# Selective scan: spreads of delta*x for four steps as four row-tiled matmuls, product with B in SBUF, decays in place in delta's ring

## What is computed

```python
deltaBC = einsum('bld,od->blo', x, W_bc)          # 64 ranks, 32 B, 32 C
dt = einsum('blr,dr->bld', deltaBC[..., :64], W_dt)
delta = softplus(dt + b_dt)
def step(h, inp):                                 # h: [b, 512, 32]
    delta_t, B_t, C_t, u_t = inp
    dA = exp(delta_t[:, :, None] * A[None])
    dBu = (delta_t * u_t)[:, :, None] * B_t[:, None, :]
    h = dA * h + dBu
    y_t = einsum('bdn,bn->bd', h, C_t)
    return h, y_t
y = scan(step) + x * D_param
```

## Time and profile before

| | |
|---|---|
| median of 3 runs | 1846.84 us (1846.28 to 1851.75) |
| the profiled execution | 1851.74 us, of it 1850.0 from the first to the last instruction |
| TensorE (PE) busy | 1758.8 us, 95% |
| VectorE (DVE) busy | 1252.1 us, 68% |
| ScalarE (ACT) busy | 1190.2 us, 64% |
| GpSimd (POOL) busy | 1194.2 us, 65% |
| mean granted TensorE clock | 0.987 of full speed |
| the scan's stage | from about 560 to 1665 us |

### The profile page before, as it was taken

The page is one execution under the profiler, slowest core; times in us unless marked ns, Lnnn a source line. Parts: engine busy times, 40 slices in busy tenths (PEclk is TensorE's granted clock), DMA queues, the critical chain, the costliest instruction groups (busy, mean ns, idle before and its releaser), DMA issues. The chain is left out here.

```text
span 1850.0 us, 26792 instructions
## 1 busy us (share of the span) xinstructions
PE 1758.8 (95%) x9472; PEld 1134.4 (61%) x9472; DVE 1252.1 (68%) x1336; ACT 1190.2 (64%) x1775; POOL 1194.2 (65%) x932
## 2 busy tenths in 40 slices
PE   7898989889989999999999999998999999999998
PEld 5666666566756556555555656554656566667886
DVE  2524252433119999789888999887999999993212
ACT  5453443498857777787767777676776767656443
POOL 4634345255617887789976997789987888772111
PEclk9999999999999999999999999999999999999999
DMA  7443323487938988789776997777878777865652
GB/s 250 133 127 96 125 76 131 134 284 249 324 121 288 314 306 274 232 287 325 242 243 214 329 318 255 243 246 263 279 262 296 249 263 273 290 237 166 210 193 91
DMA packets 159222, 427.29 MB, mean 231 GB/s; under 512 B 30992, under 2 KB 54096, under 8 KB 158704
## 3 DMA queue, kind: packets, MB, share of 16 engines
q1 hardware_dynamic: 159088, 425.57, 68.3%
HBM read 356.30 MB, written 69.21 MB: 230 GB/s over the span
## 5 line engine op out<-in xcount | busy, mean ns | idle before, releaser
L1837 POOL TENSOR_TENSOR q_or_raw_or_h_times_c<-h_states,c_rep 128x512 f32<-128x512 f32 x293 | 376.5, 1297 | 82.1 <-DVE h_states L1730 53.0
L1609 ACT ACTIVATE decay<-delta_on_states,a_neg 128x512 f32<-128x512 f32 x512 | 350.9, 716 | 23.9 <-DMA delta_on_states<-delta 22.3
L1715 DVE TENSOR_TENSOR du_spread_in_d_b<-du_spread_in_d_b,b_rep 128x1024 f32<-128x1024 f32 x256 | 310.9, 1215 | 56.1 <-PE du_spread_in_d_b L1434 55.6
L1730 DVE TENSOR_TENSOR_SCAN h_states<-decay,h_last,du_spread_in_d_b 128x512 f32<-128x512 f32 x256 | 318.4, 1270 | 7.1
L1837 POOL TENSOR_TENSOR h_times_c_rest<-h_states,c_rep 128x512 f32<-128x512 f32 x219 | 281.2, 1295 | 63.3 <-DVE h_states L1730 40.4
L1730 DVE TENSOR_TENSOR_SCAN h_states<-decay,du_spread_in_d_b 128x512 f32<-128x512 f32 x256 | 302.7, 1209 | 13.9 <-ACT h_last L1614 6.9
L1789 POOL TENSOR_TENSOR h_lo<-v_or_silu_in_h_lo,h_hi 128x512 fp32r<-128x512 f32 x128 | 166.1, 1298 | 177.0 <-ACT h_hi L1515 176.8
L111 PE MATMUL y_or_aux<-h_hi,w 128*128 128x512 f32 x468 | 223.0, 476 | 11.8 <-POOL h_lo L1789 10.5
L1434 PE MATMUL du_spread_in_d_b<-stack,selectors 96*128 96x512 bf16 x512 | 201.1, 393 | 0.3 <-DVE h_states L1730 0.3
L1680 DVE TENSOR_TENSOR v_or_silu_in_h_lo<-v_or_silu_in_h_lo,up_or_scores 128x512 f32<-128x512 f32 x128 | 86.6, 677 | 145.3 <-PE up_or_scores L113 126.6
L1515 ACT CAST h_hi<-v_or_silu_in_h_lo 128x512 fp32r<-128x512 f32 x128 | 78.9, 616 | 164.6 <-DVE v_or_silu_in_h_lo L1680 164.5
(11 more groups left out here) (235 smaller groups left out, 3862.0 us busy)
## 6 DMA issues: line engine op xcount, KB each, us to landing
delta_on_states<-delta SPq DMA_DIRECT2D x256, 512.0 KB, 5.6
w<-w_split SPq DMA_DIRECT2D x112, 512.0 KB, 5.6
attn_w_hi_or_x_hi_w<-w_split SPq DMA_DIRECT2D x112, 512.0 KB, 5.3
attn_w_lo_or_x_lo_w<-w_split SPq DMA_DIRECT2D x112, 512.0 KB, 5.2
w_split<-w_presplit_hi_lo SPq DMA_DIRECT2D x32, 512.0 KB, 3.5
w_presplit_hi_lo<-in_w13b SPq DMA_DIRECT2D x32, 256.0 KB, 3.6
w_split<-attn_w_hi_or_x_hi_w SPq DMA_DIRECT2D x8, 1024.0 KB, 6.9
w_split<-attn_w_lo_or_x_lo_w SPq DMA_DIRECT2D x8, 1024.0 KB, 6.8
```

The costliest lines, as they stand in the source:

```text
L1609: act.activation(da[:, s % ND], dring[:, s % NR], ACT.Exp, scale=a[:, column(s):column(s) + 1]).then_inc(s_da, 1)
L1715: dve.tensor_tensor(both, both, brep[:, tile_of(s // SPO) % 2].unsqueeze(1).to_broadcast([P, 2, TT]), ALU.mult).then_inc(s_db, 1)
L1730: dve.tensor_tensor_scan(hs[:, s % NH], da[:, s % ND], uu[:, s % NU], initial, ALU.mult, ALU.add).then_inc(s_hs, 1)
L1837: pool.tensor_tensor(hc[s % NC_], hs[:, s % NH], crep[:, tile_of(s // SPO) % 2], ALU.mult).then_inc(s_hc, 1)
```

## The change

- The spreads of four steps become four matmuls of 24 rows (three parts of 8), each at a row tile of its own (`tile_position=(j * 32, 0)`), into the four banks, issued together one tick ahead of the first of the four steps. They wait for the products of the four steps before, no longer for scans. `stack` is laid out anew: 12 loads per 32 steps instead of 3.
- The product with B goes from PSUM to a new ring `db` of four in SBUF; the scan reads both of its inputs from SBUF. The second product of a quad is made one step later.
- The decay is made in place in delta's ring, which grows from 6 to 10; the ring `da` goes. Loads of delta wait for scans instead of decays.
- The sum over states is issued ahead of the tick's FFN matmuls instead of ahead of their second half, right behind the spreads.
- The selectors are smaller, and the split of W2 uses two slots instead of three, with two stores instead of one and other ticks.

```diff
-PRE_TICK = (34, 58, 66, 74, 82) + tuple(126 + 22 * i for i in range(NC - 5))
+PRE_TICK = (34, 58, 70, 82) + tuple(126 + 20 * i for i in range(NC - 4))
...
-    ND, NU, NH, NC_, NR, LAG = 6, 4, 6, 7, 6, 4
-    W13, RH = 2, 6
+    NU, NH, NC_, NR, LAG = 4, 6, 7, 10, 4
+    W13, RH, LOAD_AHEAD = 2, 6, 8
...
-        da = p.sb("decay", [P, ND, TT])
+        db = p.sb("d_b", [P, NU, TT])
...
                 def pre_load(c):
                     if c:
-                        sp.wait_ge(s_bo, c)
+                        sp.wait_ge(s_bs, 32 * c)
                     sp.dma_start(pre[:, 0], w2b[:, c]).then_inc(s_bl, 16)
 
                 def pre_store(c):
                     sp.wait_ge(s_bo, c + 1)
-                    sp.dma_start(w2x[1, c // HC, :, :, c % HC].rearrange("m p s t -> p m (s t)"),
-                                 pre_hl.rearrange("p m s t -> p m (s t)")).then_inc(s_bs, 16)
+                    for i, half in enumerate((pre_hi, pre_raw)):
+                        sp.dma_start(w2x[1, c // HC, :, :, c % HC, i].rearrange("m p t -> p m t"), half).then_inc(s_bs, 16)
...
                 def stack_load(o):
                     sp.wait_ge(s_wr, 16 * (o + 1))
                     if o >= 2:
-                        sp.wait_ge(s_uu, SPO * (o - 1))
-                    for i in range(3):
-                        sp.dma_start(stk[i * 32:(i + 1) * 32, o % 2],
-                                     parts_d[o, :, i].rearrange("(j d) t -> d j t", j=JB)).then_inc(s_ld[o % 2], 16)
+                        sp.wait_ge(s_uu, QB * (o - 1))
+                    for j in range(JB):
+                        for i in range(3):
+                            rows = j * 32 + i * 2 * QD
+                            sp.dma_start(stk[rows:rows + 2 * QD, o % 2],
+                                         parts_d[o, j * 32:(j + 1) * 32, i].rearrange("(r d) t -> d r t", d=2 * QD))\
+                              .then_inc(s_ld[o % 2], 16)
 
                 def delta_load(pair):
                     s = 2 * pair
                     o, r, j = place(s)
                     if s >= NR:
-                        sp.wait_ge(s_da, s - NR + 2)
+                        sp.wait_ge(s_hs, s - NR + 2)
...
-                    if s == 0:
-                        delta_load(NR // 2)
-                    if s >= 0 and s % 2 == 0 and s + NR + 2 < STEPS:
-                        delta_load((s + NR + 2) // 2)
+                    if s >= 0 and s % 2 == 0 and s + LOAD_AHEAD < STEPS:
+                        delta_load((s + LOAD_AHEAD) // 2)
...
-                def spread_input(s):
-                    o, r, j = place(s)
-                    if s % SPO == 0:
-                        pe.wait_ge(s_ld[o % 2], 48 * (o // 2 + 1))
-                    if s >= NU:
-                        pe.wait_ge(s_hs, s - NU + 1)
-                    pe.matmul(uu[:, s % NU], sel[:, r, :], stk[:, o % 2, j]).then_inc(s_uu, 1)
+                def spread_inputs(quad):
+                    o, r, _ = place(JB * quad)
+                    if r == 0:
+                        pe.wait_ge(s_ld[o % 2], 16 * 3 * JB * (o // 2 + 1))
+                    if quad:
+                        pe.wait_ge(s_db, 2 * quad)
+                    for j in range(JB):
+                        rows = slice(j * 32, j * 32 + 3 * 2 * QD)
+                        mm = pe.matmul(uu[:, j], sel[rows, r % 2, :], stk[rows, o % 2, r // 2], tile_position=(j * 32, 0))
+                    mm.then_inc(s_uu, 1)
...
                 for tick in range(FIRST_TICK, LAST_TICK):
                     s = step_at(tick)
-                    if s == -1:
-                        spread_input(0)
-                        spread_input(1)
-                    if 0 <= s and s % 2 == 1 and s + 2 < STEPS:
-                        spread_input(s + 2)
+                    if s >= -1 and s % JB == JB - 1 and s + 1 < STEPS:
+                        spread_inputs((s + 1) // JB)
+                    if s >= LAG and (s - LAG) % JB == JB - 1 and s - LAG < STEPS:
+                        sum_states((s - LAG) // JB)
                     bank_turn(tick, 0)
                     ffn(tick, 0)
-                    if 0 <= s and s % 2 == 0 and s + 2 < STEPS:
-                        spread_input(s + 2)
                     bank_turn(tick, 1)
-                    if s >= LAG and (s - LAG) % JB == JB - 1 and s - LAG < STEPS:
-                        sum_states((s - LAG) // JB)
                     ffn(tick, 1)
...
-                    if s >= ND:
-                        act.wait_ge(s_hs, s - ND + 1)
-                    act.activation(da[:, s % ND], dring[:, s % NR], ACT.Exp,
-                                   scale=a[:, column(s):column(s) + 1]).then_inc(s_da, 1)
+                    step = dring[:, s % NR]
+                    act.activation(step, step, ACT.Exp, scale=a[:, column(s):column(s) + 1]).then_inc(s_da, 1)
...
-                    dve.wait_ge(s_uu, s + 2)
-                    both = uu[:, s % NU:s % NU + 2]
-                    dve.tensor_tensor(both, both, brep[:, tile_of(s // SPO) % 2].unsqueeze(1).to_broadcast([P, 2, TT]),
+                    dve.wait_ge(s_uu, s // JB + 1)
+                    if s >= NU:
+                        dve.wait_ge(s_hs, s + 2 - NU)
+                    dve.tensor_tensor(db[:, s % NU:s % NU + 2], uu[:, s % NU:s % NU + 2],
+                                      brep[:, tile_of(s // SPO) % 2].unsqueeze(1).to_broadcast([P, 2, TT]),
                                       ALU.mult).then_inc(s_db, 1)
...
-                    dve.tensor_tensor_scan(hs[:, s % NH], da[:, s % ND], uu[:, s % NU], initial,
+                    dve.tensor_tensor_scan(hs[:, s % NH], dring[:, s % NR], db[:, s % NU], initial,
                                            ALU.mult, ALU.add).then_inc(s_hs, 1)
...
-                    if 0 <= s + 1 < STEPS and s % 2 == 1:
+                    if s >= -1 and s % JB == JB - 1 and s + 1 < STEPS:
                         inject((s + 1) // 2)
+                    if s >= 0 and s % JB == 0 and s < STEPS:
+                        inject(s // 2 + 1)
```

More of the change, by code:

```diff
@@ L90, in __init__ @@
             q.sb("beside_second_w13", [P, KD, D])
-            self.stack = q.sb("stack", [3 * 32, 2, P // 32, TT], BF16)
+            self.stack = q.sb("stack", [P, 2, P // 32, TT], BF16)
             self.silu = q.sb("v_or_silu_in_h_lo", [P, 6, TT])
@@ L1103, in trunk_phase @@
         parts = p.sb("delta_x_parts_out", [P, 3, TT], BF16)
-        pre = p.sb("w_presplit", [P, 3, TT])
-        sel = p.sb("selectors", [3 * 32, QB, P], BF16)
-        ysel = p.sb("sum_selectors", [P, QB, 32])
+        pre = p.sb("w_presplit", [P, 2, TT])
+        sel = p.sb("selectors", [P, 2, P], BF16)
+        ysel = p.sb("sum_selectors", [P, 2 * 32 - QD])
         wdt_bsel = p.sb("w_dt_state_selectors", [P, D])
@@ L1113, in trunk_phase @@
         stk = joint.stack
-        dring = p.sb("delta_on_states", [P, NR, TT])
-        pre_hl = pre[:, 1:3].rearrange("p a t -> p (a t)").rearrange("p (m s t) -> p m s t", m=KD, s=2)
-        pre_raw = pre[:, 0].rearrange("p (m t) -> p m t", m=KD)
+        dring = p.sb("delta_on_states_or_decay", [P, NR, TT])
+        pre_raw, pre_hi = (pre[:, i].rearrange("p (m t) -> p m t", m=KD) for i in range(2))
         last = p.sb("h_last", [P, KD * SPO])
@@ L1127, in trunk_phase @@
         bank = p.ps("y_or_aux", [P, TT])
-        uu = p.ps("du_spread_in_d_b", [P, NU, TT])
+        uu = p.ps("du_spread", [P, NU, TT])
         yb = p.ps("scan_y", [P, TT])
@@ L1182, in constants @@
                 def constants():
-                    for place_, source in ((sel[:, :, :], sel_d), (ysel[:, :, :], ysel_d), (bsel[RK:P, :], bsel_d[RK:P]),
+                    for place_, source in ((sel[:, :, :], sel_d), (ysel[:, :], ysel_d), (bsel[RK:P, :], bsel_d[RK:P]),
                                            (wall[:, :, :], wall_d), (wdt[:, :], wdt_d), (feat[:, 0:2 * KD], fp_d),
@@ L1228, in w2_load @@
                     if layer:
-                        sp.wait_ge(s_bs, 16 * NC)
+                        sp.wait_ge(s_bs, 32 * NC)
                     sp.dma_start(w2[:, m].bitcast(F32), w2x[layer, unit % UNITS, m]).then_inc(s_in2[m], 16)
@@ L1301, in _ @@
                         if PARTS_STORE_AT[tick] == (0, 0):
-                            for pair in range(NR // 2):
+                            for pair in range(LOAD_AHEAD // 2):
                                 delta_load(pair)
@@ L1442, in sum_states @@
                     for j in range(JB):
-                        mm = pe.matmul(yb[j * 32:(j + 1) * 32, :], ysel[:, r, :], hc[(s + j) % NC_],
+                        mm = pe.matmul(yb[j * 32:(j + 1) * 32, :], ysel[:, 32 - QD * (r + 1):64 - QD * (r + 1)], hc[(s + j) % NC_],
                                        start=(r == 0), stop=(r == QB - 1), skip_group_check=True,
@@ L1494, in pre_centre @@
                     act.wait_ge(s_bl, 16 * i + 16)
-                    if i:
-                        act.wait_ge(s_bs, 16 * i)
```

(19 more changed lines are left out.)

## The result

The changed kernel takes **2158.11 us** (median of 4 runs, 2156.91 to 2160.76) against 1847.67: 1.1675 times as long, 95% interval 1.1662 to 1.1689 (the ratios here and below can differ by 0.001 from the quotients of the medians). Forecast were 2210, range 2110 to 2390. The profiled execution took 2157.07 us, its span 2155.3.

What follows compares the result with a forecast made beforehand. TensorE was taken to bound the scan stage, VectorE near second; afterwards scans and GpSimd take turns at a shared port: 563 + 584 + 274 + 47 makes the stage 1468 us, plus 363, so 2210 us, range 2110 to 2390.

Steps and rivals of the forecast that it cites:

- The bounds: Scan stage, 1105 of 1850 us: TensorE ends last in most places, VectorE a near second at 7.6 to 7.8 us per quad.
- part 1: Spreads on TensorE: four row tiles side by side cost 0.33 to 0.42 us instead of 0.94, saving 67 to 78 us.
- Part 2: Product with B to SBUF: scans then have two SBUF inputs and exclude GpSimd operations, in turns; stage plus 363 us.
- Costs at nothing: The product with B writing SBUF instead of PSUM: no cost, plus or minus 5 us in the stage.
- The sum: Port time in the scan stage: scans 563, GpSimd behind scans 584, other GpSimd 274, plus 47 idle: stage 1468 us.
- The floor: Scan stage with GpSimd and scans alone filling the shared port: 1421 us against 1105, plus 316 at least.
- the waits for ScalarE and TensorE: GpSimd's 95 us of idle time in the stage not spent on scans stays; scans fill about half, so +47 us.
- The upper bound by whole durations: Scan stage with no start-up hidden and no idle filled: scans 636, GpSimd 917, idle 95, together 1648 us, plus 543.
- The smaller edits: Decays in place, extra stack loads, split stores and the early sum over states: nothing added to the time.
- The clock: TensorE's granted clock could fall where it waits; with 3 us of slack per quad no cost unless half clock becomes the rule.
- Rival (a): Scan stage: scans don't exclude GpSimd and TensorE's saving counts: -40 us, 1807 us, between 1760 and 1840; chance 0.11.

Runs made afterwards that it cites:

- experiment 4: Changed kernel with the product with B left in place in PSUM, so a quad's spreads wait for the four scans before: 1900.91 us, ratio 1.0283.
- experiment 2: Kernel before with decays in place in delta's ring (8 slots) and the product with B to SBUF, spreads one by one: 2173.6 us, ratio 1.1754.
- experiment 6: Changed kernel with the product in place in PSUM and spreads in twos, each two waiting for scans of their own banks: 1838.96 us, ratio 0.9942.
- experiment 3: Kernel before with decays in place in delta's ring (8 slots) and only each quad's first product to SBUF: 1983.89 us, ratio 1.0728.
- experiment 5: GpSimd's product with C cut to 8 of 512 columns from the eighth step: changed kernel 1881.41 us, kernel before with the same cut 1837.94 us.

## Why the prediction was right

**The bounds and part 1** held in the mechanism: tiles run side by side. Four spreads cost 0.31 us, a little under the forecast 0.33 to 0.42, and TensorE's busy time fell by 80 us in experiment 4 (forecast 67 to 78). The forecast gave nothing of this to the time; by experiment 2 all the rest of the change together is worth 15 us. The price of a change of tiling was 0.10 us each way in my sum; on the way out it is 0.20, as experiment 6 shows. It drops out for four spreads beside the sum, since they share that exit.

**Part 2** was the decision, carried over from tensor-tensor operations to the scan, and experiments 2 and 3 confirm it for the scan itself. "Costs at nothing" for the product's destination: minus 15 ns x 256 = 4 us, inside the 5.

**The sum.** The floor was 1421 us for the stage and the forecast 1468; measured were 1415, 6 us under the floor. Counting in the trace, 421 GpSimd operations are over 1.5 us, that is, in turn with a scan; 421 x 2.16 = 909 us, 309 others x 1.25 = 386, and 91 scans that held nobody up x 1.10 = 100, together 1396, so some 20 us of idle port (16 us by the records themselves). Two terms were mis-sized and both made me too high: a turn is 2.16 us, not 1.10 + 1.14 = 2.24, since after a wait a scan of either kind and a GpSimd operation all take 1.08 us, where I had 1.07, 1.13 and 1.14. And the waits for ScalarE and TensorE, of which I let 47 us stand, were mostly filled: GpSimd waited for the two some 20 us in the stage, against some 90 in the kernel before. Here the other waits of a user of the port nearly vanished once the port was the bound. The upper bound by whole durations (1553 without waits) is 138 us off: it counts as held what is start-up.

Two readings of the prediction were off and don't enter its sum. Short operations of VectorE are 968 - 512 - 256 = 200 in the stage, 1.6 per quad and not 1.4. And L1707 wasn't the only operation with two SBUF inputs there: L1703 at 607.07 has them too, and ran while GpSimd was idle.

The Trainium skill, "SBUF — State Buffer", section "SBUF: two separate sides", has the rule that decided this; the trace agrees on which operations exclude each other, and differs on "for the whole instruction": a turn takes 2.16 us where the two durations sum to 1.27 + 1.29 = 2.56.

**The smaller edits** stayed invisible, as costed. **The clock**: 0.90 in the stage against 0.99. TensorE waited up to 10.6 us at a time for GpSimd's products; from 1008 to 1016 us, where it stood 10.58 us, the granted clock is 0.50, the lower of its two levels (1.2 of 2.4 GHz). No run separates the clock, but the waits speak for its being hidden: in the stage VectorE waits 50 us for TensorE and GpSimd 6, against 63 and 52 in the kernel before at 0.99. The rows are, in this order, the table of stretches, TensorE's timeline and the waits of the changed kernel:

```profile
1008.00:1016.00 8.00, 2.66 (x10) 0.91 (x11) 7.76 (x6) 1.85 (x2) 8.00 (x5) 0.50 0.34 132
...
1013.34 1.07 PE L1446 MATMUL scan_y<-q_or_raw_or_h_times_c,sum_selectors 128*32 128x512 f32 x2 [10.58 <-POOL h_times_c_rest L1835]
...
PE scan_y L1446 <- POOL h_times_c_rest L1835: 54.1, 16, 10.6
```

**Rival (a)** had one thing right that I want to keep: without exclusion a lighter TensorE need not shorten the stage. Experiment 4 shows TensorE 80 us lighter and the kernel 53 us slower, by waits of VectorE that its order of spreads brings.

## What to carry to other kernels

Before moving an operand of a VectorE operation from PSUM to SBUF, count its SBUF inputs: with two, scans and tensor-tensor operations took turns here with GpSimd's tensor-tensor operations on SBUF, and where both engines are busy the sum of the holds is the estimate of the stage (1421 us for 1415 measured). One long outlier in a duration column (679/691/2896 in the earlier trace rows) is the place to look for it, even where the line is cheap. Row tiles paid where they stood beside other tiled matmuls; alone among full ones, two side by side cost as much as two in a row.

## What the runs showed of the hardware

- A scan (`TENSOR_TENSOR_SCAN`) with both inputs in SBUF is about as fast as one from PSUM when no GpSimd operation holds it up (1191 and 1187 ns at the least), and in turns with GpSimd a pair takes 2.16 us.
- Very short GpSimd operations take part too. In experiment 5 the products of 8 columns take 0.20 us in the median, but 183 of the 505 take over 1.0 us, at most 1.27: they wait for a whole scan. (The 2211 in the first row is one of the seven products that kept their 512 columns.) The rows are the product's durations, one that waits, the scan that it waits for, and one that doesn't wait:

```profile
L1836 POOL TENSOR_TENSOR q_or_raw_or_h_times_c<-h_states,c_rep x293: 193/203/2211, 555.4 to 1692.3; 128x8 f32<-128x8 f32 x145, 128x512 f32<-128x512 f32 x2
...
1554.02 1.27 POOL L1836 TENSOR_TENSOR q_or_raw_or_h_times_c<-h_states,c_rep 128x8 f32<-128x8 f32 x1
1554.02 1.28 DVE L1726 TENSOR_TENSOR_SCAN h_states<-delta_on_states_or_decay,h_last,d_b 128x512 f32<-128x512 f32 x1
1555.37 0.20 POOL L1836 TENSOR_TENSOR h_times_c_rest<-h_states,c_rep 128x8 f32<-128x8 f32 x1
```

- Four row tiles of 24 rows and 512 columns start together and take the array for 0.31 us; leaving a tiling for full matmuls costs about 0.2 us, entering 0.1.
